# Attention in a one-core kernel: the pieces of V moved in front of the projections in each unit's full-array stretch

## What is computed

```python
q = jnp.einsum('ntc,hdc->nhtd', x_q, w_q)          # 16 heads of 64
k = jnp.einsum('ntc,hdc->nhtd', x_q, w_k)
v = jnp.einsum('ntc,hdc->nhtd', x_q, w_v)
a = jnp.einsum('nhtd,nhsd->nhts', q, k) / math.sqrt(q.shape[3])
a = jnp.where(causal_forbidden[None, None], -jnp.inf, a)
a = jax.nn.softmax(a, axis=3)
y = jnp.einsum('nhts,nhsd->nthd', a, v).reshape(a.shape[0], t, -1)
return y @ w_o
```

## Time and profile before

| | |
|---|---|
| median of 3 runs | 2182.37 us (2179.69 to 2184.25) |
| the profiled execution | 2176.84 us, of it 2175.1 us span |
| PE busy | 2089.7 us, 96% of the span |
| DVE, POOL, ACT busy | 1411.5, 1384.2, 933.3 us |
| mean granted clock of TensorE | 0.991 |
| attention on PE (L1482, first to last start) | 638.0 to 1723.6 us |

### The profile page before, as it was taken

One profiled execution on the slowest core, in us unless ns is written; L12 is line 12 of the kernel. 1 busy time (PEld: TensorE's weight loads), 2 busy tenths in 40 slices (PEclk: granted clock), 3 DMA queues, 4 the chain that ended last, 5 costly groups with the idle time before them and its releaser, 6 DMA issues.

```text
span 2175.1 us, 37200 instructions
## 1 busy us (share of the span) xinstructions
PE 2089.7 (96%) x13666; PEld 1627.2 (75%) x13666; DVE 1411.5 (65%) x3215; ACT 933.3 (43%) x1780; POOL 1384.2 (64%) x1242
## 2 busy tenths in 40 slices
PE   7998999999899999999999999999999899999998
PEld 5446888889786676767667766667666588899997
DVE  7375697676647666466766467875867546976554
ACT  6202543444344455335544244542544425444443
POOL 4313686677447787547777367763867947777774
PEclk9998999999999999999999999999999999999999
DMA  4523554555230011011010111101100144545552
GB/s 136 188 97 104 154 124 110 136 153 144 63 98 30 21 37 33 12 48 61 29 49 11 39 40 59 40 21 39 45 16 1 60 155 124 139 113 128 131 149 34
DMA packets 133795, 172.42 MB, mean 79 GB/s; under 512 B 16872, under 2 KB 109040, under 8 KB 133616
## 3 DMA queue, kind: packets, MB, share of 16 engines
q1 hardware_dynamic: 109040, 136.47, 19.3%
q0 software_dynamic: 24576, 33.57, 9.2%
HBM read 130.03 MB, written 39.85 MB: 78 GB/s over the span
## 4 chain that ended last, share of the span: by engine, by line
PE 69%; DVE 9%; POOL 7%; issue 3%; ACT 2%; DMA 1%; SPq 1%; POOLq 0%; DVEq 0%; ACTq 0%
PE psum L1354 13%; PE psum L1375 11%; PE psum L1505 9%; PE psum L1482 9%; PE psum L1425 7%; PE psum L1533 5%; POOL t_acc L2487 5%; PE psum L1439 4%; PE psum L1450 3%; PE psum L1487 3%; PE psum L1518 2%; DVE f_hlo L2225 1%; DVE f_hhi L2223 1%; DVE f_wlo L2196 1%; DVE f_junk L2065 1%
## 5 line engine op out<-in xcount | busy, mean ns | idle before, releaser
L2487 POOL TENSOR_TENSOR t_acc<-t_acc,t_p 128x1024 f32<-128x1024 f32 (+3 forms) x256 | 421.6, 1647 | 25.2
L1796 ACT ACTIVATE t_p<-psum 128x512 f32<-128x512 f32 (+3 forms) x768 | 321.6, 496 | 65.6 <-PE psum L1487 54.2
L2404 POOL TENSOR_TENSOR f_wlo<-f_wst,f_whi 128x256 fp32r<-128x256 f32 x256 | 221.3, 941 | 166.3 <-ACT f_whi L1723 166.2
L1375 PE MATMUL psum<-f_whi,f_hhi 128*128 128x256 f32 x992 | 286.3, 289 | 7.6 <-DVE f_hlo L2225 7.6
L1375 PE MATMUL psum<-f_whi,f_hlo 128*128 128x256 f32 x992 | 280.5, 283 | 0.0
L1375 PE MATMUL psum<-f_wlo,f_hhi 128*128 128x256 f32 x992 | 280.2, 282 | 0.0
L2223 DVE CAST f_hhi<-f_h 128x512 fp32r<-128x512 f32 x256 | 140.1, 547 | 212.8 <-ACT f_h L1743 212.3
L1743 ACT ACTIVATE f_h<-psum 128x512 f32<-128x512 f32 x256 | 153.1, 598 | 283.2 <-PE psum L1354 271.0
L2501 POOL TENSOR_TENSOR t_yT<-t_pvs,t_den 128x512 f32<-128x512 f32 x64 | 83.1, 1298 | 287.1 <-ACT t_pvs L1806 256.3
L1505 PE MATMUL psum<-t_p,t_v 128*64 128x512 f32 (+3 forms) x1536 | 259.0, 486 | 0.0
L1505 PEld LDWEIGHTS psum<-t_p,t_v 128*64 128x64 f32 x1536 | 109.3, 137 | 160.2 <-issue 149.2
(11 more groups left out here) (301 smaller groups left out, 4786.0 us busy)
## 6 DMA issues: line engine op xcount, KB each, us to landing
f_wst<-in_L_ffn_w SPq DMA_DIRECT2D x64, 1024.0 KB, 4.9
t_wk<-wkT SPq DMA_DIRECT2D x32, 256.0 KB, 3.6
t_wq<-wqT SPq DMA_DIRECT2D x32, 256.0 KB, 3.8
t_wv<-wvT SPq DMA_DIRECT2D x16, 512.0 KB, 4.9
normal<-f_xy SPq DMA_DIRECT2D x5, 1024.0 KB, 6.1
a_x<-in_L_attn_a_x SPq DMA_DIRECT2D x4, 1024.0 KB, 7.7
res<-a_x SPq DMA_DIRECT2D x32, 128.0 KB, 2.7
t_xy<-res SPq DMA_DIRECT2D x4, 1024.0 KB, 6.1
```

The source lines that it names most:

```text
L1375: m = pe.matmul(out, h[:, js], w[:, f, :], start=(f == 0 and a == 0 and j % 2 == 0), stop=(f == FT - 1 and a == 2), skip_group_check=True)
L1796: act.activation(p[:, i, :], k.bank[bank][:, q0:], ACT.Exp, scale=1.0 / float(np.sqrt(k.DH))).then_inc(k.drained[bank], 1)
L2404: m = pool.tensor_tensor(t["wlo"][n % 2][:, i, ks], t["wst"][:, i, ks], t["whi"][n % 2][:, i, ks].bitcast(F32), ALU.subtract)
L2487: pool.tensor_tensor(acc[:, :, q0:], (p0 if kt == 1 else acc)[:, :, q0:], p[:], ALU.add).then_inc(k.p_acc, 1)
```

## The change

The pieces of V of a unit's full-array stretch are issued first, in front of the four projections and of the turning of the maxima. Number, kind and operands of all of them stay. Where the stretch begins with the transposes of a new sequence (u % 8 = 6) there are no pieces of V, and nothing changes. So 28 of the 32 units are touched.

```diff
         def full_array(u):
 
+            first = (u + 2) % NHP and value_pieces((u + 1) % NHP)
+            for _ in range(first):
+                next(state["values"])
+                yield
             if u + 2 < U:
                 if (u + 2) % NHP == 0:
                     yield from prepare((u + 2) // NHP)
                 yield from project(u + 2, 0, 2, 1, 3)
             else:
                 pump(state["route"])
             self.max_rows(u + 1)
-            for _ in range(value_pieces((u + 1) % NHP)):
+            for _ in range(value_pieces((u + 1) % NHP) - first):
                 next(state["values"])
                 yield
             ready()
```

## The result

The changed kernel takes 2185.22 us (median of 20 runs, 2183.22 to 2187.47) against 2179.44 us of the kernel before (20 runs too): ratio 1.0025, 95% interval 1.0019 to 1.0032. By the ratio that is 5.5 us (4.1 to 7.0), 0.25%; the two medians differ by 5.8. Forecast were +5.2 us and +0.24%, 2187.6 us from the median then shown; "slower by over 0.2%" had the largest chance, 0.55.

What follows compares the result with a forecast made beforehand. TensorE, busy 2089.7 of 2175.1 us, was taken to bound the kernel. Terms 0 + 4.5 + 1.1 - 1.2 + 0.8 gave +5.2 us, 2187.6 us from the median; range 2181 to 2191.5.

Steps and rivals of the forecast that it cites:

- seams, ordinary units: Joins between moved pieces in ordinary stretches: unchanged to 0.05 us per unit, sum 0, bounds -2.8 to +2.8 us.
- units 9, 12, 17, 25: `t_neg` falls behind the wait for GpSimd's power in VectorE's full queue, delaying TensorE 1.13 us each: +4.5 us.
- units 10, 18: Chunk 0's sums need bank 6 from the last projection; TensorE waits 0.5 to 0.55 us, twice: +1.1 us.
- unit 20: Copies that TensorE transposes come right behind the last maximum, so the first transpose starts earlier: -1.2 us.
- unit 26: Threshold wait goes (0.8 with semaphore), chunk 0's values wait 1.6 us for bank 1: +0.8 us.
- rival of slack in VectorE's chain: Units 9, 12, 17 and 25: VectorE has spare time, only +0.7 us is left, total 2183.1 us; chance 0.16.
- collision with GpSimd's product: Row instruction beside GpSimd's product, units 9, 12, 17, 25: assumed to stay; rival without it 4 x 0.92 us less, chance 0.05.
- A second such wait stays: Unit 20: TensorE's second wait for copies to transpose remains, since they stand behind a low part as before.
- The wait for the ranks (2.86) stays: Unit 26: TensorE's 2.86 us wait remains, with 4.53 us from transpose to ranks before and after.
- The clock's cost: Unit 26: low clock for 3.3 us behind the ranks' wait, costing 1.65 us, left in; +-1.7 us.
- VectorE in ordinary units: 0: Later low parts and `t_neg` cost nothing in ordinary units, covered by the 10 us column stretch: 0.
- one clock stretch more or less: Rival: one low-clock stretch added or missing, total 2189.3 or 2185.9 us; chance 0.11.

Runs made afterwards that it cites:

- e4: V first only in touched units without a norm at the stretch's start, gate scores or ranks, all else as in the kernel before; ratio 1.0005 to it.
- e1: Changed kernel, but units 9, 12, 17 and 25 keep the old order; ratio 1.0010 to the kernel before.
- e2: Kernel before with V first in units 9, 12, 17 and 25 alone; ratio 1.0027 to the kernel before.
- e3: Changed kernel, but in units 9, 12, 17, 20 and 25 `t_neg` stands ahead of `norm_rows` in VectorE's queue; ratio 1.0009 to the kernel before.
- e7: Changed kernel plus six short VectorE instructions directly in front of `t_neg` in units 9, 12, 17 and 25; ratio 1.0043 to the kernel before.
- e8: Kernel before plus six short VectorE instructions directly in front of `t_neg` in units 9, 12, 17 and 25; ratio 0.9991 to the kernel before.
- e5: Changed kernel with other banks for the last projection in units 10 and 18 and the turned maxima in unit 26; ratio 0.9994 to the kernel before.
- e6: Kernel before with V first in units 20 and 26 alone and bank 2 for unit 26's turned maxima; ratio 0.9976 to the kernel before.
- e9: Changed kernel with `t_neg` ahead of `norm_rows` in units 9, 12, 17, 20, 25 and other banks in 10, 18, 26; ratio 0.9986 to the kernel before.
- e12: Kernel before with V first in units 20 and 26, two empty steps ahead of the ranks and three more ahead of `norm_rows`; ratio 0.9959 to the kernel before.
- e10: Kernel before with two empty steps between comparison and ranks, so that the ranks come in unit 27; ratio 0.9979 to the kernel before.

## Why the prediction was right

The direction and the main mechanism were right; that the size agrees to 0.3 us is partly luck (units 20, 26, 29 and 30 below). Point by point, forecast and measured, us:

| term | forecast | trace | shown by |
|---|---|---|---|
| seams, ordinary units | 0 | +0.1 over 18 units | e4 |
| units 9, 12, 17, 25 | +4.5 | +4.6 | e1, e2, e3, e7, e8 |
| units 10, 18 | +1.1 | +1.3 | e5 |
| unit 20 | -1.2 | -1.7 | e6 |
| unit 26 | +0.8 | +0.85 | e5 |
| units 29, 30 | 0 | +0.1 (+0.8 waiting, -0.7 clock) | runs with V first in unit 29 against those without |
| sum | +5.2 | +5.2 | 5.5 measured |

- *Norm units.* The mechanism and the size, 1.13 each, are what the runs show: 1.12 to 1.19. The rival of slack in VectorE's chain is refuted by e7, where a further 0.78 us arrives in full. The collision with GpSimd's product stayed (1.65 us in unit 9), so its rival didn't come up.
- *Units 10 and 18.* The bank was the cause. Of 0.65 us, e5 gives back 0.54. The rest was not in my working and I can't place it.
- *Unit 20.* Mis-sized. The first transpose starts 3.45 us into the stretch, forecast 3.55, before 4.60. Its wait is 0.31 and not the forecast 0.6, since V ended later than my 3.0. "A second such wait stays" was right, but it fell by 0.48, since the copies (L2052, 128x256) took 0.69 us and not 1.18. Before, they ran from 1348.91 on beside GpSimd's addition of 1348.26 to 1349.54; in the changed kernel, at 1354.65, they were nearly done when the next addition began (1355.29). I had kept a duration without asking which neighbour it has in the new place.
- *Unit 26.* The sum was right through two errors of 0.6 us that cancel. "The wait for the ranks (2.86) stays" was wrong: it fell to 2.25. Of this, 0.23 us come from a low part (`t_qlo`, at 1568.91) that before stood between the transpose and the copy of the thresholds (0.54 us behind the transpose, now 0.31). The rest is the copy and the four comparisons, which took 3.84 us before (the long ones 1.94 and 1.29, each beside an addition of GpSimd) and 3.46 now (a single long one, 2.38). And `t_neg` cost 2.2 and not 1.6: I worked it out from an idle VectorE, but VectorE's work behind the ranks, up to 1583.60 (a product of 1.74 us at 1580.38 in it), kept the low parts back. The clock's cost stayed in, as assumed, at another place (1.57 before, against e8; 1.75 now).
- *Units 29 and 30.* Here the step "VectorE in ordinary units: 0" failed. I took the column stretch as the cover for the late low parts and `t_neg`, and in unit 29 routing work fills it: +0.78 in its column stretch and +0.43 in the next row halves, less some 0.4 in unit 30's column stretch (12.0 for 12.4 us without low clock), +0.8 in all. It doesn't show in the sum because the trace of before has a low-clock stretch in unit 30 that costs 0.7 and the changed one has none. I had priced such a stretch as a rival, "one clock stretch more or less", and it came in part. Without it the trace would say about +5.9; the measured 5.5, with 4.1 to 7.0, fits both.

## What to carry to other kernels

Where the bounding engine's own work doesn't change, go through what stands next to the moved pieces: which instruction is queued behind a wait on another engine, and which bank, by a ring that goes on counting, now meets a use with a fixed bank. Both are repaired without giving up the order (e9; unit 29's queue was not), and a wait in a queue costs only if something that is needed soon stands behind it (e3 against e7, e12). And look at what the trace of before waits for in that part: the largest gain here, 4.6 us in e10 (3.0 without the clock's part), had nothing to do with the change. When two single traces agree with a sum, compare their low-clock stretches before you believe it: here one more or less is worth 0.7 to 1.7 us.

## What the runs showed of the hardware

- The granted clock fell to 0.50 (1.2 GHz) for 3.4 us at places that no wait alone decides. With the order of before in unit 26, TensorE waited 2.83 to 2.86 us for the ranks; the kernel before and e2 have the low clock behind it, and e8 the full 2.4 GHz. In unit 26 the changed kernel waited 2.25 us for the ranks and was granted the full 2.4 GHz behind it, and 1.2 GHz behind the next wait of 2.00; e5 has the same 2.26 and no low stretch in the unit; e7 has one behind three waits of about 1.9 us and none behind the fourth. What decided is not settled by these runs.
- The price of such a stretch depends on what it meets: 1.7 us in the weighted values, 1.6 in projections, 0.85 in e7's row halves, 0.7 in unit 30, and nothing in front of another wait (unit 22).
- A short VectorE instruction can last as long as GpSimd's beside it. VectorE and GpSimd of the changed kernel in unit 26, ahead of the ranks:

```profile
1575.46 0.21 DVE L2102 TENSOR_TENSOR e_ge<-e_pr,e_Tb 128x64 bf16<-128x64 f32 x1
1575.60 2.38 DVE L2101 TENSOR_TENSOR e_ge<-e_pr,e_Tb 128x64 bf16<-128x64 f32 x1
```

```profile
1575.55 2.35 POOL L2491 TENSOR_TENSOR t_acc<-t_acc,t_p 128x1024 f32<-128x1024 f32 x1
```

The second of the four comparisons, of 64 columns, took 0.21 us. The third began 0.05 us behind GpSimd's addition and ended with it, after 2.38. The Trainium skill (SBUF — State Buffer, "Who interferes with whom") says that a VectorE instruction with two inputs in SBUF contends with a GpSimd instruction that reads SBUF, as its second input comes through the read interface that the two share. By that rule, the trace agrees: the comparisons read `e_pr` and `e_Tb`, the addition `t_acc` and `t_p`. By my estimate, the 2.38 us less the 0.21 of the free one, this is most of TensorE's 2.25 us of waiting here.
